# A delta-rule and LoRA-quantised block kernel: a product between the two X products of an inversion level, and the LoRA factors loaded in another order

## The reference, cut to what matters

```
q, v = x@Wq+bq, x@Wv+bv;  k = normalised(x@Wk+bk)
alpha, beta, gate = sigmoid(x@Wa+ba), sigmoid(x@Wb+bb), sigmoid(x@Wg+bg)
S = a*(S - b*(S k) k^T) + b*v k^T;   o = (q^T S) * gate      # per step, S is 128x128
x = layernorm(x + o@Wo+bo)                                    # layer 1: delta rule
w_l = (q_l/7.5 - 1)*scale_l + lb_l@la_l                       # layer 2: 6 linears 512x512,
x = layernorm(x + three blocks of (linear, LN, gelu, linear) + residual)   # LoRA rank 32
x = layernorm(x)                       # layer 3: its attention adds nothing (v has no columns)
x = layernorm(x + gelu((x@U1)@V1+b1)@U2@V2+b2)                # layer 4
```

## Time and profile before

| what | us |
|---|---|
| median of 3 runs | 2344.09 |
| lowest and highest of them | 2342.64, 2344.79 |
| the profiled execution | 2342.25 |
| its span, first to last instruction | 2340.3 |
| its delta stage, up to PE's first instruction of the next part | 629.8 |
| PE busy in the span | 2277.4 |
| ACT busy, DVE busy, POOL busy | 1197.2, 1537.8, 786.7 |

### The profile page before, as it was taken

One profiled execution on the slowest core, in us unless ns is written; L12 is line 12 of the kernel. 1 busy time (PEld: TensorE's weight loads), 2 busy tenths in 40 slices (PEclk: granted clock), 3 DMA queues, 4 the chain that ended last, 5 costly groups with the idle time before them and its releaser, 6 DMA issues.

```text
span 2340.3 us, 37476 instructions
## 1 busy us (share of the span) xinstructions
PE 2277.4 (97%) x12223; PEld 1914.8 (82%) x12223; DVE 1537.8 (66%) x2938; ACT 1197.2 (51%) x2367; POOL 786.7 (34%) x1329
## 2 busy tenths in 40 slices
PE   7999999997799999999999999999999999999997
PEld 6999999996688888888888888888888788888886
DVE  3666666665675766766667667576676766666666
ACT  4455455554544344353353334434435577777775
POOL 3555555564311211112111111121111235555555
PEclk9999999998899999999999999999999999999999
DMA  5122212243300202002012030020221323333322
GB/s 139 55 91 95 102 66 86 99 144 97 124 1 19 90 1 73 36 18 90 0 35 73 0 108 0 18 90 0 72 67 36 144 73 108 108 108 108 108 90 72
DMA packets 101735, 166.38 MB, mean 71 GB/s; under 512 B 19664, under 2 KB 22480, under 8 KB 101520
## 3 DMA queue, kind: packets, MB, share of 16 engines
q1 hardware_dynamic: 97328, 163.69, 20.6%
q10 hardware_dynamic: 4320, 1.71, 0.3%
HBM read 115.05 MB, written 50.33 MB: 71 GB/s over the span
## 4 chain that ended last, share of the span: by engine, by line
PE 70%; DVE 1%; POOL 1%; issue 0%; ACT 0%; POOLq 0%; DVEq 0%
PE quant_bank L1553 7%; PE quant_bank L1554 7%; PE quant_bank L1552 7%; PE quant_bank L1942 6%; PE quant_bank L1944 6%; PE quant_bank L1943 6%; PE quant_bank L1579 5%; PE quant_bank L1580 5%; PE quant_bank L1581 5%; PE quant_bank L1569 4%; PE quant_bank L1598 3%; PE quant_bank L1600 3%; PE quant_bank L1599 3%; PE quant_bank L1541 1%; PE quant_bank L1959 1%; PE quant_bank L1610 1%
## 5 line engine op out<-in xcount | busy, mean ns | idle before, releaser
L1393 POOL TENSOR_SCALAR quant_var<-quant_mv 128x1 f32<-128x1 f32 x256 | 55.5, 217 | 1007.3 <-DVE quant_mv L1468 1007.3
L1421 ACT ACTIVATE quant_g_hi<-quant_bank,kept_beta,kept_gamma 128x512 fp32r<-128x512 f32 x192 | 150.2, 782 | 395.8 <-PE quant_bank L1569 395.8
L1552 PE MATMUL quant_bank<-kept_W_hi,quant_h_hi 128*128 128x512 f32 x768 | 305.5, 398 | 0.0
L1553 PE MATMUL quant_bank<-kept_W_lo,quant_h_hi 128*128 128x512 f32 x768 | 303.6, 395 | 0.0
L1554 PE MATMUL quant_bank<-kept_W_hi,quant_h_lo 128*128 128x512 f32 x768 | 303.4, 395 | 0.0
L1466 DVE BATCH_NORM_STATS2 quant_stats<-quant_bank 128x6 f32<-128x512 f32 x192 | 133.9, 698 | 190.9 <-PE quant_bank L1554 190.9
L1907 DVE TENSOR_TENSOR mlp_g_lo<-quant_bank,mlp_g_hi 128x512 fp32r<-128x512 f32 x256 | 176.3, 689 | 105.0 <-ACT quant_bank L1844 105.0
L1843 ACT ACTIVATE mlp_g_hi<-quant_bank,mlp_b 128x512 fp32r<-128x512 f32 x256 | 177.2, 692 | 71.1 <-PE quant_bank L1944 63.8
L1579 PE MATMUL quant_bank<-quant_g_hi,kept_W_hi 128*128 128x512 f32 x512 | 205.2, 401 | 0.0
L1580 PE MATMUL quant_bank<-quant_g_hi,kept_W_lo 128*128 128x512 f32 x512 | 202.6, 396 | 0.0
L1581 PE MATMUL quant_bank<-quant_g_lo,kept_W_hi 128*128 128x512 f32 x512 | 202.5, 395 | 0.0
(11 more groups left out here) (283 smaller groups left out, 5860.5 us busy)
## 6 DMA issues: line engine op xcount, KB each, us to landing
delta_x_in<-L_attn_x_d SPq DMA_DIRECT2D x16, 1024.0 KB, 7.9
delta_x_res<-L_attn_x_d SPq DMA_DIRECT2D x16, 1024.0 KB, 5.6
x_d<-delta_z SPq DMA_DIRECT2D x64, 256.0 KB, 2.1
kept_x_in<-x_d SPq DMA_DIRECT2D x16, 1024.0 KB, 5.3
quant_y<-x_d SPq DMA_DIRECT2D x16, 1024.0 KB, 5.3
x_d<-quant_y SPq DMA_DIRECT2D x16, 1024.0 KB, 5.1
mlp_x_in<-x_d SPq DMA_DIRECT2D x16, 1024.0 KB, 10.4
mlp_x_res<-x_d SPq DMA_DIRECT2D x16, 1024.0 KB, 6.7
```

Of the source, the lines that this page charges most:

```text
L1421: nc.scalar.activation(g_hi[m][:, k, :], tr[k][:, :], ACT.Gelu, bias=beta[:, b, k:k + 1], scale=gamma[:, b, k:k + 1])
L1552: mm(out, x_hi, W_hi[2 * b][:, k, :], start=False, stop=False, skip_group_check=True)
L1553: mm(out, x_hi, W_lo[2 * b][:, k, :], start=False, stop=False, skip_group_check=True)
```

## The change

Four edits, all in the delta stage.

1. `ORDER`, levels 1 to 5: one of the two output products of a level (`attn`), which stood behind `X.i.1` (in some levels behind a DVE piece too), now stands between `X.i.0` and `X.i.1`. In level 6, `attn.3.2'` stands between `inverse.0` and `inverse.1` instead of ahead of both. As `ORDER_PREVIOUS` and `ORDER_LAST` are built from it, all units follow.
2. The `lb` transfer moves from behind the last residual load to the start of the program, ahead of the scales. The pieces `lb_hi` and `lb_lo` move from `ORDER_LAST` to `ORDER_PREVIOUS`, that is one unit earlier.
3. SP: the last residual load is issued ahead of the four stores of unit (6,1), behind a wait for that unit's last `z`. The `la` transfer is issued straight after these stores, ahead of `load_rows(3)`.
4. `la_hi.0` moves from level 2 to level 3 of the last unit, `la_hi.1` from level 3 to `stats.0` of the same level, where `la_lo.0` stays.

```diff
@@ ORDER @@
-            Y.1.0 T.1.0 Y.1.1 T.1.1 attn.0.0' X.1.0 X.1.1 attn.0.1' g.6
-            Y.2.0 T.2.0 Y.2.1 T.2.1 attn.0.2' X.2.0 X.2.1 z.0' attn.1.0' g.7
+            Y.1.0 T.1.0 Y.1.1 T.1.1 attn.0.0' X.1.0 attn.0.1' X.1.1 g.6
+            Y.2.0 T.2.0 Y.2.1 T.2.1 attn.0.2' X.2.0 attn.1.0' X.2.1 z.0' g.7
...
-            Y.6.0 T.6.0 Y.6.1 T.6.1 attn.3.1' attn.3.2' inverse.0 inverse.1 g.11 gout.0 z.3'""")
+            Y.6.0 T.6.0 Y.6.1 T.6.1 attn.3.1' inverse.0 attn.3.2' inverse.1 g.11 gout.0 z.3'""")
@@ ORDER_PREVIOUS @@
-            ("kh", 0, 0): dequants((0, 2), (0, 3))})
+            ("kh", 0, 0): dequants((0, 2), (0, 3)),
+            ("X", (2, 1), 0): [("lb_hi", 0, 0)],
+            ("X", (3, 1), 0): [("lb_hi", 1, 0)],
+            ("X", (4, 1), 0): [("lb_hi", 2, 0), ("lb_lo", 0, 0)]})
@@ ORDER_LAST @@
-            ("X", (2, 0), 0): [("la_hi", 0, 0)],
             ("X", (2, 1), 0): dequants((2, 1)),
-            ("X", (3, 0), 0): [("la_hi", 1, 0)],
-            ("stats", 0, 1): [("la_lo", 0, 0), ("lb_hi", 0, 0), ("lb_hi", 1, 0)],
-            ("X", (4, 0), 0): dequants((2, 2)) + [("lb_hi", 2, 0), ("lb_lo", 0, 0)],
+            ("X", (3, 0), 0): [("la_hi", 0, 0)],
+            ("stats", 0, 1): [("la_lo", 0, 0), ("la_hi", 1, 0)],
+            ("X", (4, 0), 0): dequants((2, 2)),
@@ sync, ahead of all rounds @@
+            sp.dma_start(lb[:, :, :], q["lora_b"].rearrange("l (k p) r -> p (l k) r", p=P)).then_inc(w_["lb_in"], 16)
             sp.dma_start(scale[:, :, :, :], q["scales"].rearrange("l (k p) g -> p l k g", p=P)).then_inc(w_["scale_in"], 16)
@@ sync, end of the stage @@
             load_rows(2)
+            sp.wait_ge(z_done[GB - 1], GROUPS * CHUNKS - 2)
+            load_residual(CHUNKS - 1, 1)
             store(CHUNKS - 2, 1)
-            load_residual(CHUNKS - 1, 1)
-            sp.dma_start(lb[:, :, :], q["lora_b"].rearrange("l (k p) r -> p (l k) r", p=P)).then_inc(w_["lb_in"], 16)
             sp.wait_ge(s_["g_ps"], GROUPS * CHUNKS)
+            load_la(la_st_early, slice(0, EARLY), "la_early_in")
             load_rows(3)
-            load_la(la_st_early, slice(0, EARLY), "la_early_in")
             store(CHUNKS - 1, 0)
```

More of the change, by code:

```diff
@@ L304, in delta_rule_and_weights @@
             part.2 part.3 part.4 part.5 part.6 kA.0 qA.0 norm.2'' norm.3''
-            Y.1.0 T.1.0 Y.1.1 T.1.1 attn.0.0' X.1.0 X.1.1 attn.0.1' g.6
-            Y.2.0 T.2.0 Y.2.1 T.2.1 attn.0.2' X.2.0 X.2.1 z.0' attn.1.0' g.7
-            Y.3.0 T.3.0 Y.3.1 T.3.1 attn.1.1' X.3.0 X.3.1 stats.0' attn.1.2' g.8
-            Y.4.0 T.4.0 Y.4.1 T.4.1 attn.2.0' X.4.0 X.4.1 z.1' attn.2.1' g.9
-            Y.5.0 T.5.0 Y.5.1 T.5.1 attn.2.2' X.5.0 X.5.1 z.2' stats.1' attn.3.0' g.10
-            Y.6.0 T.6.0 Y.6.1 T.6.1 attn.3.1' attn.3.2' inverse.0 inverse.1 g.11 gout.0 z.3'""")
+            Y.1.0 T.1.0 Y.1.1 T.1.1 attn.0.0' X.1.0 attn.0.1' X.1.1 g.6
+            Y.2.0 T.2.0 Y.2.1 T.2.1 attn.0.2' X.2.0 attn.1.0' X.2.1 z.0' g.7
+            Y.3.0 T.3.0 Y.3.1 T.3.1 attn.1.1' X.3.0 attn.1.2' X.3.1 stats.0' g.8
+            Y.4.0 T.4.0 Y.4.1 T.4.1 attn.2.0' X.4.0 attn.2.1' X.4.1 z.1' g.9
+            Y.5.0 T.5.0 Y.5.1 T.5.1 attn.2.2' X.5.0 attn.3.0' X.5.1 z.2' stats.1' g.10
+            Y.6.0 T.6.0 Y.6.1 T.6.1 attn.3.1' inverse.0 attn.3.2' inverse.1 g.11 gout.0 z.3'""")
         def dequants(*tiles):
```

## The result

The changed kernel takes **2321.12 us** (median of 5 runs, 2320.67 to 2322.98) where the kernel before takes 2344.09: ratio 0.9908, 95% interval 0.9897 to 0.9920. The forecast was 2320 (2312 to 2333). The profiled execution is one of 2320.67 us with a span of 2318.7.

What follows compares the result with a forecast made beforehand. PE's queue was taken to bound the looped units, and ACT's wait for la the last. 12.6 less 0.7 and 12.0 made -23.9 us: from the median 2344.09 to 2320 us, range 2312 to 2333.

Steps and rivals of the forecast that it cites:

- What bounds: PE's queue sets the looped units' time; in the last unit PE idles 11.96 us while ACT waits for la.
- Edit 1, 0.18 us a level: Output product between X products removes X.i.1's wait for ACT's copy: 0.18 us in 70 levels, 12.6 us.
- 0.08 left: Margin in each level: first half's sum on DVE ends at 315.96, the Y reading it starts at 316.15.
- Level 6 gives back 0.05 a unit: inverse.0 loses one of two products covering ACT's longer copy: 0.05 us in 14 units, 0.7 us.
- Edits 3 and 4: Last unit: earlier la replaces 12 us wait at X.3.0 by about 2 at X.4.0; about -12 us, bounds -9 and -14.
- The half of DVE's 0.85: Last unit: 0.85 us from a slow dequant beside POOL's la_lo.0 in level 4; half counted as gone.
- Full clock there: Sign expected in the last unit: PE at full granted clock, where before it read 0.50 after the idle time.
- Nothing, and no gain either: Start of program: lb ahead of the scales delays x rows' issue from 29.79 to 34.5, read at 83.16; no effect.
- TAIL shifted whole: Everything behind level 6 starts from the same point, so TAIL moves earlier as one, keeping the gain.
- The chains did fill part of the gap: Rival: margins vanish, levels stay at 2.2 us, only the last unit gains, 2332; only one gain either way: 0.18.
- la wasn't late: Rival: la lands at 567.5, PE waits 4.4 us at X.4.0, clock falls, 2323; included in the 0.74 for both gains.
- PE paid no weight loads: Rival: each level pays two exposed loads of 0.19 us, +26.6, with the last unit 2359; slower had 0.04.

Runs made afterwards that it cites:

- e3: Changed kernel with Y's two waits (DVE's sum, masked matrix) in the other order in levels 2 to 6: 2322.10 us.
- e4: Changed kernel with la issued ahead of the last two stores of unit (6,1): 2318.95 us, ratio 0.9896.
- e6: Changed kernel with lb late again: loaded right ahead of la, its three ACT pieces in the last unit: 2326.52 us, ratio 0.9928.
- e8: e4 with norm.0 behind level 5's copies and both dequants behind the second sum in the last unit: 2319.66 us, ratio 0.9899.
- e9: The changed kernel measured once more, nothing altered: 2324.09 us, ratio 0.9914.
- e5: Changed kernel with rows 3 issued ahead of la again, the residual still ahead of the stores: 2328.51 us, ratio 0.9940.

## Why the prediction was right, and where not

- **What bounds.** Right: PE's distances in the looped units and ACT's wait for la in the last. B and C hold 21.2 of the 21.6 us.
- **Edit 1, 0.18 us a level.** The mechanism was right, the size in the loop wasn't: 0.146. `X.i.1` waits no longer. The failed step is the margin: "0.08 left" for the first half's sum. I counted from the end of the sum to the load and left out the step from the semaphore to the load, 0.12 us where that wait stands on an instruction of its own. Y's second pass then starts 0.03 late (e3). In the two written-out units the step is 0.05, nothing is late, and the level gained 0.175. So 60 x 0.146 and 10 x 0.175 are 10.5 instead of 12.6.
- **Level 6 gives back 0.05 a unit.** About right: a looped unit is 0.66 us shorter where five levels gave 0.73, so 0.07. In all -9.6 in B instead of -11.9; that is the main miss, 2.3 us.
- **Edits 3 and 4.** Right: on the old clock `X.4.0` stands at 566.53 (556.79 plus 9.74), forecast 566.7, and la came 4.6 us behind its last issue, forecast 5.5. That it fits so closely is luck: the last issue stands at 560.38 on the old clock, forecast 559.6, and the two errors cancel. C gained 11.55, forecast 12.0. The half of DVE's 0.85 that I counted didn't come: the wait before the Y that follows `X.4` is gone, but level 4 to 5 stayed at 3.17 (3.22), since PE was at the lower clock there.
- **"Full clock there"** was wrong: 0.50 in 558 to 560. By the estimate at e4 it cost about 1 us, more than the 0.4 us by which C missed its forecast.
- **Edit 2, "Nothing, and no gain either"**, was half right. The start shows no cost (A 37.24 against 37.37). But late lb costs 5.4 us (e6): I had it inside edit 3's 11.6 without seeing that either alone doesn't give them.
- **TAIL shifted whole.** Right to 0.4 us in D, in this pair of profiles. e8 shows that it was luck of size: TAIL follows POOL's chain and only moved because that chain moved. In e9, the same kernel, D is 1.6 us longer than before.
- **Rivals.** The chains did fill part of the gap, 0.03 of 0.18 in the loop. la wasn't late, PE paid no weight loads (X passes 273 ns at the median).
- **The median**: two sets of after are 2321.12 and 2324.09, so the nearness of 2320 is partly luck. The sum over B and C, -21.2 against -23.9, is the fair measure of it.

## What to carry to other kernels

A product between two short ones hides the copy that the second waits for, and what it really brings is set by the next chain, read with the step from semaphore to weight load in it; a wait that ends last belongs on the instruction that needs it, and which of two waits stands there can differ between a loop and written-out code (e3), so read both. A transfer that a chain waits for goes ahead of every larger or finely cut one in its queue, and the work behind the chain, `norm.0` and POOL here, is late next. Judge gains below the run-to-run spread from stretches that repeat, and not from the whole time; and see that the stretch ends on the chain that the rest follows (e8).

## What I had not expected of the hardware

- The wait for a semaphore costs 0.12 us from the end of DVE's sum to the start of the weight load when it stands on a register instruction ahead of the product, and 0.06 when it stands on the product; in written-out code 0.05 became 0.12 by the same edit (e3).
- la's three copies to 32 partitions, 768 KB, land 3.5 to 4.6 us behind their issues with 1024 KB of rows behind them (after), and 7.2 to 10.4 us with these rows ahead (e5). The rows land in 7.4 us behind la and in 10.1 us ahead of it: so both are slower in that order.
- In the last unit PE's waits of 1.19 and 0.62 us (e4) are followed by full clock, and those of 1.75, 2.00, 2.23 and 3.53 us by the lower one. In TAIL, with waits of up to 2.6 us, the same kernel meets the lower clock in one run and not in the next, which makes 2.3 of the 3.4 us between two profiles of it (after and e9).
